# A fused gelu on ScalarE, and one weight block moved out of the token stage of an attention and feed-forward kernel

## What is computed

```python
x = x + attention(conditioned(x))        # routed keys: 32 of 64 a head, softmax, 16 heads of 32
h = x @ W.T + adapter_delta(x)           # low-rank adapter chosen per sequence
gate = h @ dequant(gate_packed, gate_scales).T      # 512 -> 4096, 4-bit codes
up   = h @ dequant(up_packed, up_scales).T
gelu = tanh(0.7978845608028654 * (gate + 0.044715 * gate**3)) * gate * 0.5 + gate * 0.5
x = x + (gelu * up) @ dequant(down_packed, down_scales).T
```

## Time and profile before

| | |
|---|---|
| median of 3 runs | 2802.58 us |
| the profiled execution | 2798.91 us |
| its span, first to last instruction | 2797.3 us |
| TensorE busy | 2663.4 us, 95% |
| VectorE busy | 2213.4 us, 79% |
| ScalarE busy | 1225.8 us, 44% |
| POOL busy | 1008.1 us, 36% |
| mean granted TensorE clock | 0.987 of full |
| first step of the feed-forward stage | about 758 us |

### The profile page before, as it was taken

One profiled execution on the slowest core, in us unless ns is written; L12 is line 12 of the kernel. 1 busy time (PEld: TensorE's weight loads), 2 busy tenths in 40 slices (PEclk: granted clock), 3 DMA queues, 4 the chain that ended last, 5 costly groups with the idle time before them and its releaser, 6 DMA issues.

```text
span 2797.3 us, 54265 instructions
## 1 busy us (share of the span) xinstructions
PE 2663.4 (95%) x19200; PEld 2448.9 (88%) x19200; DVE 2213.4 (79%) x3708; ACT 1225.8 (44%) x2409; POOL 1008.1 (36%) x1189
## 2 busy tenths in 40 slices
PE   5888998998899999999999999999999999999998
PEld 5777887887789999999999999999999999999998
DVE  6887888888578888888888888888888888756555
ACT  4444545445344444444444444444444444444443
POOL 3454444534334343433444253433344343300000
PEclk8999999999899999999999999999999999999999
DMA  3232222322776697678667766966786686657542
GB/s 116 70 106 97 93 92 85 105 91 91 269 283 222 223 358 260 233 255 329 227 249 292 286 236 230 369 241 225 270 324 248 219 329 256 242 210 279 192 191 86
DMA packets 197576, 599.87 MB, mean 214 GB/s; under 512 B 21224, under 2 KB 80488, under 8 KB 185200
## 3 DMA queue, kind: packets, MB, share of 16 engines
q1 hardware_dynamic: 162160, 496.89, 48.6%
q0 software_dynamic: 35328, 101.82, 9.7%
HBM read 417.83 MB, written 180.75 MB: 214 GB/s over the span
## 4 chain that ended last, share of the span: by engine, by line
PE 71%; DVE 17%; issue 4%; ACT 3%; POOL 3%; DMA 2%; SPq 0%; DVEq 0%; POOLq 0%; ACTq 0%
PE bank_a L902 22%; PE down L910 22%; PE bank_b L902 12%; PE proj L725 6%; PE bank_c L902 6%; DVE inter L1450 2%; DVE inter L1441 1%; DVE rope_sin L1287 1%; ACT k_diagonal L1026 1%; DVE rope_in L1286 1%; DVE lut_line L1237 1%; DMA out<-x 1%; DVE inter_parts L1457 1%; DVE rope_sin L1284 1%; PE scores L769 1%
## 5 line engine op out<-in xcount | busy, mean ns | idle before, releaser
L902 PEld LDWEIGHTS bank_a<-h_in,gu_slot 128*128 128x128 f32 x6144 | 855.7, 190 | 74.2 <-ACT copy_p L1186 9.3
L902 PE MATMUL bank_a<-h_in,gu_slot 128*128 128x256 f32 x6144 | 899.1, 282 | 6.1 <-ACT copy_p L1186 6.1
L910 PE MATMUL down<-d_slot,inter_parts 128*128 128x512 f32 x3072 | 835.8, 394 | 2.0 <-DVE inter_parts L1457 2.0
L910 PEld LDWEIGHTS down<-d_slot,inter_parts 128*128 128x128 f32 x3072 | 527.6, 190 | 68.8 <-DVE inter_parts L1457 2.4
L902 PE MATMUL bank_b<-h_in,gu_slot 128*128 128x256 f32 x3072 | 456.4, 284 | 17.2 <-DVE up_val L1463 17.2
L594 POOL TENSOR_TENSOR lut_v<-lut_v,signed_scale 128x512 f32<-128x512 f32 x96 | 123.8, 1290 | 865.5 <-DVE lut_v L1253 865.3
L902 PEld LDWEIGHTS bank_b<-h_in,gu_slot 128*128 128x128 f32 x3072 | 404.5, 192 | 24.7 <-DVE up_val L1463 24.7
L1188 ACT ACTIVATE gate_val<-bank_a 128x256 f32<-128x256 f32 x256 | 98.3, 384 | 429.4 <-PE bank_a L902 429.4
L1437 DVE TENSOR_TENSOR up_val<-bank_b,copy_p 128x256 f32<-128x256 f32 x256 | 108.3, 423 | 205.8 <-PE bank_b L902 205.8
L1457 DVE TENSOR_TENSOR inter_parts<-inter,inter_parts 128x512 fp32r<-128x512 f32 x256 | 203.6, 795 | 33.3 <-ACT inter_parts L1154 33.3
L579 POOL TENSOR_TENSOR w_parts<-lut_v,w_parts 128x512 fp32r<-128x512 f32 (+1 forms) x160 | 224.4, 1402 | 13.1
(11 more groups left out here) (127 smaller groups left out, 3739.6 us busy)
## 6 DMA issues: line engine op xcount, KB each, us to landing
h_in<-h_scratch SPq DMA_DIRECT2D x64, 3584.0 KB, 12.9
acc<-out SPq DMA_DIRECT2D x64, 1024.0 KB, 5.4
out<-acc SPq DMA_DIRECT2D x64, 1024.0 KB, 4.3
gu_slot<-w_scratch SPq DMA_DIRECT2D x32, 1792.0 KB, 10.1
w_scratch<-w_parts POOLq DMA_DIRECT2D x96, 512.0 KB, 6.7
h_scratch<-h_out SPq DMA_DIRECT2D x32, 896.0 KB, 5.1
d_scratch<-w_parts POOLq DMA_DIRECT2D x32, 512.0 KB, 3.4
d_slot<-d_scratch SPq DMA_DIRECT2D x32, 512.0 KB, 15.6
```

The costliest lines, as they stand in the source:

```text
L902: ins = pe.matmul(bank[:, 0:HALF], lhsT, rhs, start=(start and n == 0), stop=(n == len(pairs) - 1), skip_group_check=True)
L910: ins = pe.matmul(down[tc][:].rearrange("p (k h) -> p k h", k=2), inter_parts[:, j % 2, u, tc * P:(tc + 1) * P], d_slot[j][:, :, v, :], st ...
```

## The change

ScalarE evaluates the gelu of the gate in one instruction (`Gelu_apprx_tanh`) into `inter`, at the place where the square was. The square, the tanh and two of VectorE's four passes of that chain (`gate_inner`, and the first of `gelu_times_up`) are gone; the pass that is left multiplies by `up_val`. The new instruction also waits until `inter_low` of the step before (`inter_ready`) has read `inter`. `EARLY` becomes 2: iterations 0 to 11 dequantise one unit each, 12 to 15 none. In the feed-forward stage a step takes (2, 2) operations, sixteen a tile, so a block takes three tiles, and 14 blocks take the first 42 tiles; 22 tiles are left with none.

```diff
-        EARLY = 3
-        SLOTS = [2 if t < 2 else 1 for t in range(NT)]
+        EARLY = 2
+        SLOTS = [1 if t < 6 * EARLY else 0 for t in range(NT)]
...
-                store_rest(*UNITS[t - 1][-1])
-                scale_unit(*UNITS[t][0])
+                    if UNITS[t - 1]:
+                        store_rest(*UNITS[t - 1][-1])
+                if UNITS[t]:
+                    scale_unit(*UNITS[t][0])
...
-            store_unit(*UNITS[NT - 1][-1])
-            store_rest(*UNITS[NT - 1][-1])
...
-            def square(n, b):
+            def gelu(n, b, first=False):
                 act.wait_ge(gate_first, n + 1)
                 act.wait_ge(gate_second, n + 1)
-                act.activation(gate_sq[:], gate_val[:, b], ACT.Square).then_inc(sq_done, 1)
-
-            def tanh(n):
-                act.wait_ge(gin_done, n + 1)
-                act.activation(inter[:], inter[:], ACT.Tanh, scale=GELU_SCALE * GELU_CUBIC).then_inc(tanh_done, 1)
+                if not first:
+                    act.wait_ge(inter_ready, n)
+                act.activation(inter[:], gate_val[:, b], ACT.Gelu_apprx_tanh).then_inc(gelu_done, 1)
...
-                        square(n - 1, 1 - b)
+                        gelu(n - 1, 1 - b, first and j == 1)
...
-            def gate_inner(n, b):
-                dve.wait_ge(sq_done, n + 1)
-                dve.scalar_tensor_tensor(inter[:], gate_sq[:], 1.0 / GELU_CUBIC, gate_val[:, b], ALU.add, ALU.mult).then_inc(gin_done, 1)
...
-            def gelu_times_up(n, b):
-                dve.wait_ge(tanh_done, n + 1)
-                dve.scalar_tensor_tensor(inter[:], inter[:], 1.0, gate_val[:, b], ALU.add, ALU.mult).then_inc(gval_done, 1)
-                dve.wait_ge(gval_done, n + 1)
+            def gelu_times_up(n):
+                dve.wait_ge(gelu_done, n + 1)
                 dve.wait_ge(up_first, n + 1)
-                dve.scalar_tensor_tensor(inter[:], inter[:], 0.5, up_val[:], ALU.mult, ALU.mult).then_inc(inter_done, 1)
+                dve.tensor_tensor(inter[:], inter[:], up_val[:], ALU.mult).then_inc(inter_done, 1)
...
-            OPS = [(2, 2), (2, 0), (0, 2), (2, 2)]
+            OPS = [(2, 2), (2, 2), (2, 2), (2, 2)]
...
-            def four_tiles(quarter, block_c=None, first=False):
...
+            def six_tiles(f, first=False):
+                for r in range(6):
+                    ffn_tile(f * 3 + r // 2, r % 2, first=(first and r == 0), block_c=f * 2 + EARLY + r // 3, turn=r % 3)
```

More of the change, by code:

```diff
@@ L38 @@
 MASKED = -1.0e30
-GELU_CUBIC = 0.044715
-GELU_SCALE = 0.7978845608028654
 HI, LO = 0, 1
@@ L1193, in _ @@
             n_last = NG * NF * NS - 1
-            square(n_last, 1)
-            tanh(n_last)
+            gelu(n_last, 1)
             parts_free(NG * NF, 0)
@@ L1367, in iteration, with unit @@
                 it = t
-                first, second = UNITS[t][0], (UNITS[t] + [None])[1]
+                def unit(first, last):
+                    for c, k in UNITS[t]:
+                        dequantise(c, k, first, last)
                 value(it, 0)
@@ L1371, in iteration @@
                 softmax_shift(t, 0)
-                dequantise(*first, 0, 4)
+                unit(0, 4)
                 if do_tail:
@@ L1381, in iteration @@
                     mixed(t + 1)
-                dequantise(*first, 4, DQ - 2)
+                unit(4, DQ - 2)
                 softmax_sum(t, 1)
@@ L1385, in iteration @@
                 heads_low(t, 0)
-                dequantise(*first, DQ - 2, DQ)
-                if second is not None:
-                    dequantise(*second, 0, 4)
+                unit(DQ - 2, DQ)
                 if do_head:
@@ L1392, in iteration @@
                     hidden_low(t - 1, 0)
-                if second is not None:
-                    dequantise(*second, 4, DQ)
                 add_residual(it, t, 0)
@@ L1504, in ffn_tile @@
                     o = dequantised(o, OPS[j][1])
[L1506 to L1515 removed]
+            def six_tiles(f, first=False):
+                for r in range(6):
+                    ffn_tile(f * 3 + r // 2, r % 2, first=(first and r == 0), block_c=f * 2 + EARLY + r // 3, turn=r % 3)
+            SIXES = (NCP - EARLY) // 2
+            assert 3 * PER_TILE == 6 * DQ and 2 * SIXES == NCP - EARLY
+            six_tiles(0, first=True)
+            with dve.Fori(1, SIXES) as f:
+                six_tiles(f)
+            with dve.Fori(3 * SIXES, NG * NF // 2) as f:
+                ffn_tile(f, 0)
+                ffn_tile(f, 1)
             i_last = NG * NF - 1
@@ L1518, in _ @@
             up_from_a22(n_last)
-            gate_inner(n_last, 1)
-            gelu_times_up(n_last, 1)
+            gelu_times_up(n_last)
             inter_low(n_last, 1)
```

23 lines of the change are left out of this document (3 added, 20 removed).

## The result

The changed kernel takes 2806.2 us (median of 20 runs, 2801.47 to 2811.02), the kernel before 2802.1 us beside it (20 runs): a ratio of 1.0018, 95% interval 1.0012 to 1.0025. I had forecast 2759 us. Nothing was gained; the interval lies just above 1, so that the change costs 0.1 to 0.25% if anything. The profiled execution has a span of 2805.5 us where before has 2797.3, 8.2 us more.

A forecast was written before the change was run, and what follows sets the result against it. The feed-forward stage, three quarters of the span, was taken as bound by TensorE's matmuls plus stalls behind VectorE during dequantisation. -28.3 + 10 - 2.0 - 23 = -43.3 us from 2798.9 gave 2755.6, forecast as a 2759 us median, range 2744 to 2779.

The forecast's parts named there:

- The two passes fewer: Feed-forward stage: two VectorE passes less per step remove the stall that comes with dequantisation, -28.3 us over 208 steps.
- The gelu's price: ScalarE, feed-forward step: the gelu takes 0.63 us, like the square on the same tile, and costs nothing.
- The table load: ScalarE, second feed-forward step: one load of 1283 ns, hidden where ScalarE idles 3.18 us for a DMA store, cost 0.
- The end: Program's end: TensorE's idle wait before the last twelve matmuls goes, -2.0 us.
- The quicker dequantisation: Feed-forward stage: POOL's long units, now given two steps, make VectorE and sometimes TensorE wait, +10 us, between 0 and 25.
- POOL's lock: Rival, feed-forward stage: POOL's port lock slows VectorE's passes, so half the old stalls stay, +14 us, 2773 us; 10 in 100.
- POOL sets the pace: Rival, operation 7 of units 4 and 0: all 28 long units take 20.3 us, 2831 us; 4 in 100.
- The token stage: Token stage: six units fewer save 23 us, bounds 12 and 27.
- (a): Token stage, iteration 0: without its second unit the first residual is no longer held, -5.5 us.
- (b): Token stage, iteration 1: the residual comes as early as in an ordinary iteration, -4 us.
- (c): Token stage: three long iterations (4, 6 and 10) instead of five, -11.5 us.
- (d): Token stage: one unit off an ordinary iteration saves 0.5 us for each of four.

The follow-up runs named there:

- e7: e1 with 60 empty instructions at the very start of VectorE's program, nothing else changed: 2774.71 us, ratio 0.9900.
- e3: The changed kernel with a buffer and semaphore of its own for the last store of a long unit: 2760.91 us, ratio 0.9846.
- e1: The kernel before with only the gelu in one instruction, on its old dequantisation schedule: 2806.8 us, ratio 1.0014.
- e9: The kernel before with 210 empty instructions at VectorE's start and nothing else: 2849.59 us, ratio 1.0171.
- e5: The changed kernel with no unit in the token-stage iterations after a long unit, and POOL's store deferred there: 2784.58 us, ratio 0.9934.
- e11: The changed kernel with e5's slots, unevenly dealt operations, e3's buffer and VectorE's six-tile loop written out: 2736.53 us, ratio 0.9773.

## Why the prediction was wrong

I forecast -43.3 us from the profiled execution's time; it was +8.1. Point by point:

- **The two passes fewer**, -28.3: right. It is 27.4 us, and e7 shows it alone. That `up_from_s3` gets time to spare holds where nothing else new stands ahead of it.
- **The gelu's price** (0.63 us from the square's row): right, 632 ns. **The table load** (0): nearly right, but not by the cover that I had named. The load stands at the start of the second step, ahead of that idle time, and TensorE waits 0.47 us at 751.32 for the copy behind it; the same product had no wait before. By the Trainium skill, ScalarE: Activation LUTs (What ACT_TABLE_LOAD costs), a drain was to come on top; the trace doesn't show one: the load starts 0.07 us after `gate_second` ends, and the gelu starts as the load ends.
- **The end**, -2.0: right, -1.7.
- **The quicker dequantisation**, +10 with bounds of 0 and 25: this is the step that failed. It took POOL's time for a long unit as fixed, and did not see that the unit holds a wait for its own store to land. The term measured 52.9 us, of four parts.
  - I had "tiles 8, 24 and 32", 3 x 2.7 us. There were eight such events, 32.0 us: tiles 8, 9, 15, 23, 24, 32, 33 and 39, so the last of a group, its first and its second. They stand behind the eight long units that took 19.4 us and more; no other took 18. I had one row of a long unit at a group's start (20.3 us) and took the cause to be `h_in`'s load. It is the landing of the unit's own store while a group's weights are loaded. I had seen POOL's duration, not the wait inside it. The trace of before has one long unit of 18.0 to 20.2 us at each of six group boundaries, so it could have been read there.
  - Each cost 4.0 us, not 2.7. The wait at S3 itself was 2.5 us in the mean (19.7 in all), so its price was about right. What I had at nothing is TensorE's clock: with six of the eight waits it was granted at 0.50 for 3.4 us, about 10.2 us of these 32.0.
  - "0.1 us for each of 25" was 18.5 us in all, 13.4 of them in third steps. I had called the third step "even": one pass gone, two half passes new. Beside POOL's next unit one of these halves takes 1.41 us in place of 0.28 and the multiplication 1.87 in place of 0.69. The order alone doesn't do it: e3 keeps it and loses nothing there. It takes a long unit that ends late. My rival of POOL's lock had named the slowed passes, at +14 us.
  - 2.4 us is the jump back at tile 24, with 14.7 us of waits at VectorE. Nothing in the trace of before pointed to it. e1 and e9 show that it can be 26 to 39 us in the schedule of before.
- My upper bound for this step, 25 us, was "a wait as long as the whole slack". A wait has no such bound: what is past the slack goes to TensorE in full, and the clock can add to it. The rival "POOL sets the pace" had the place right, operation 7 behind a long unit, and that more transfers would make it late. I gave it 4 in 100 because I asked whether all 28 units are that long, where eight of them at twice its price of 1.9 us, with the small stalls, were enough.
- **The token stage**, -23: it gave 14.7. (a) and (b) came as worked out, -4.3 and -4.4 against -5.5 and -4, but the first scores were 1.4 us later. (c) was right, -11.5. (d), -0.5 for each of four, gave nothing. Iteration 12 got 3.4 us longer; "no operation waits for it" was true of VectorE's operations, but POOL's work on the keys stands behind that store. Iteration 4 got 1.0 us longer. e5 confirms the reason for 4, 6 and 10; for iteration 12 it doesn't, so the account above names what stood there, not a cause that is shown.

## What to carry to other kernels

When a producer is given less time, look inside its span for waits on transfers, and take their length at the worst place of the program, not at a typical one; a second buffer, or uneven spacing, can be worth more than the change itself (here 45 us). Compare the slack with the wait in each place: below the slack it costs nothing (e7: 18 waits, no stall), above it the excess is paid, and TensorE's clock may fall behind it, which is paid too; look at the granted clock behind each long wait. A large unrolled loop body is sensitive to where it lies in the engine's code; look at the instruction queue's packets and at waits for "issue" before an edit is judged, since a shift of the code alone gave 32 us in one kernel here (e7) and took some 26 from another (e9).

## What the hardware showed that I had not expected

- A jump back over 289 to 478 instructions of VectorE cost it 2.9 to 4.7 us on average and 7.0 us at most, or nothing at all, by its place in the code (e1, e7, e9). TensorE lost 38.6 us by it in e1, 23.1 of them idle at `bank_b`.
- TensorE's granted clock was 0.50 for 3.4 us with six of the eight long waits at S3 in the changed kernel (1.75 to 3.55 us of idle time), and stayed at 1.00 with the other two (1.62 and 2.68 us). I put the cost at 10.2 us in all. The kernel before, with waits under 1 us, and e7 and e11, with none, have no such stretch behind the first steps.
- An empty VectorE instruction that only raises a semaphore took 0.10 to 0.12 us (21.7 us for 210, 7.4 us for 60).
- The work that waited for a 512 KB store from POOL's queue began 15.1 us behind its issue where a group's loads run; the median of the 96, from issue to landing, is 4.9 us on the changed kernel's page.
